# Gated linear attention and a mixture of experts on one core: score steps in four quarters, sums of squares in pieces, and the first expert tile's head inside the last attention slot

## The reference

```python
q = _l2norm((x @ Wq).reshape(Bb, Tt, H, DK))
k = _l2norm((x @ Wk).reshape(Bb, Tt, H, DK))
v = (x @ Wv).reshape(Bb, Tt, H, DV)
alpha = jax.nn.sigmoid(x @ Wg).reshape(Bb, Tt, H, DK)

def step(S, qkva):
    q_t, k_t, v_t, a_t = qkva
    S = a_t[..., None] * S + k_t[..., None] * v_t[:, :, None, :]
    o_t = jnp.einsum('bhkv,bhk->bhv', S, q_t)
    return (S, o_t)
...
x = _layernorm(x + o @ Wo)
x = _layernorm(x + ffn(x))
```

## Time and profile before

| | |
|---|---|
| time, median of 3 runs | 1812.88 us (1812.57 to 1818.45) |
| the profiled execution | 1823.8 us, span 1822.0 us |
| TensorE, matmuls | 1699.3 us busy (93%), 35591 |
| TensorE, weight loads | 1401.9 us busy (77%), 35591 |
| VectorE | 1453.9 us busy (80%), 3326 |
| ScalarE | 1074.1 us busy (59%), 2352 |
| GpSimd | 610.8 us busy (34%), 470 |
| instruction queue | 283 packets, 4.64 MB |

### The profile page before, as it was taken

The page is one execution under the profiler, slowest core; times in us unless marked ns, Lnnn a source line. Parts: engine busy times, 40 slices in busy tenths (PEclk is TensorE's granted clock), DMA queues, the critical chain, the costliest instruction groups (busy, mean ns, idle before and its releaser), DMA issues.

```text
span 1822.0 us, 81575 instructions
## 1 busy us (share of the span) xinstructions
PE 1699.3 (93%) x35591; PEld 1401.9 (77%) x35591; DVE 1453.9 (80%) x3326; ACT 1074.1 (59%) x2352; POOL 610.8 (34%) x470
## 2 busy tenths in 40 slices
PE   6999999999999999999999999999978999999996
PEld 5888878878888788887887888878857777777775
DVE  4888788787878888787877887877857888888886
ACT  5666555655665556655665565655536666666663
POOL 3322232232322232232323222222204554555544
PEclk9999999999999999999999999999989999999998
DMA  7000000000000000000000000000002322223311
GB/s 215 4 9 10 3 10 3 10 4 10 4 9 10 3 9 4 9 4 9 3 10 9 4 9 4 9 4 9 4 14 98 116 82 94 105 71 117 103 67 64
DMA packets 38129, 60.80 MB, mean 33 GB/s; under 512 B 3080, under 2 KB 24848, under 8 KB 37776
## 3 DMA queue, kind: packets, MB, share of 16 engines
q1 hardware_dynamic: 37776, 55.59, 9.1%
HBM read 46.93 MB, written 4.46 MB: 28 GB/s over the span
## 4 chain that ended last, share of the span: by engine, by line
PE 68%; DVE 14%; issue 8%; ACT 5%; DMA 3%; DVEq 0%; POOL 0%; SPq 0%; ACTq 0%; POOLq 0%
PE bank L539 8%; PE bank L672 8%; PE bank L627 7%; PE bank L541 7%; PE bank L540 7%; PE bank L682 5%; PE bank L658 5%; PE bank L630 5%; PE bank L579 5%; PE bank L589 4%; PE bank L646 3%; DVE kt_sb L1510 3%; PE bank L615 3%; DVE v_sb L1517 3%; DMA ew_raw<-cw_dram 2%
## 5 line engine op out<-in xcount | busy, mean ns | idle before, releaser
L471 POOL TENSOR_TENSOR rn_sb<-ss_sb,expo 128x8 f32<-128x8 f32 x128 | 213.5, 1668 | 785.1 <-DVE ss_sb L1272 785.1
L1227 DVE TENSOR_TENSOR qq_sb<-qq_sb,tot_sb 128x512 f32<-128x512 f32 (+1 forms) x384 | 264.5, 689 | 188.1 <-PE bank L627 149.5
L1227 DVE TENSOR_TENSOR k_sb<-k_sb,tot_sb 128x512 f32<-128x512 f32 (+1 forms) x384 | 321.9, 838 | 5.3 <-PE bank L630 5.1
L997 ACT ACTIVATE at_sb<-diag_sb 32x256 f32<-32x256 f32 x256 | 106.0, 414 | 170.6 <-DVE diag_sb L1239 165.9
L972 ACT ACTIVATE v_sb<-bank,rn_sb 128x128 f32<-128x128 f32 x512 | 139.7, 384 | 83.0 <-PE bank L541 80.1
L627 PEld LDWEIGHTS bank<-qq_sb,k_sb 128*32 128x32 f32 x12288 | 128.7, 110 | 58.4 <-issue 43.6
L627 PE MATMUL bank<-qq_sb,k_sb 128*32 128x16 f32 x12288 | 149.8, 185 | 22.3 <-issue 20.5
L961 ACT ACTIVATE a_sb<-bank 128x512 f32<-128x512 f32 x128 | 76.5, 598 | 154.2 <-PE bank L541 145.6
L672 PE MATMUL bank<-v_sb,at_sb 128*128 128x128 f32 x1024 | 151.5, 291 | 5.0 <-issue 2.5
L539 PE MATMUL bank<-wg_hi,ew_hi 128*128 128x512 f32 x320 | 135.2, 423 | 20.1 <-DVE v_sb L1517 20.1
L507 POOL TENSOR_TENSOR wq_lo<-v_sb,wq_hi 128x512 fp32r<-128x512 f32 x80 | 111.9, 1403 | 114.4 <-ACT wq_hi L1120 114.4
(11 more groups left out here) (191 smaller groups left out, 4291.0 us busy)
## 6 DMA issues: line engine op xcount, KB each, us to landing
ew_raw<-cw_dram SPq DMA_DIRECT2D x32, 768.0 KB, 6.4
x_nat<-in_L_attn_x_dram SPq DMA_DIRECT2D x16, 256.0 KB, 3.1
x_nat<-x_all SPq DMA_DIRECT2D x16, 256.0 KB, 2.5
ew_raw<-cw_dram SPq DMA_DIRECT2D x16, 256.0 KB, 3.7
e_sb<-cw_dram SPq DMA_DIRECT2D x16, 256.0 KB, 7.1
out_dram<-k_sb SPq DMA_DIRECT2D x16, 256.0 KB, 2.3
ew_raw<-in_L_ffn_exp_w_dram SPq DMA_DIRECT2D x3, 512.0 KB, 5.1
qq_sb<-in_L_attn_Wq_dram SPq DMA_DIRECT2D x1, 512.0 KB, 3.7
```

What stands on the lines that cost most here:

```text
L471: nc.gpsimd.tensor_tensor(rn_sb[par][:, i, :, :].rearrange("p h c -> p (h c)"), ss_sb[:, i * G:(i + 1) * G], expo[:, 0:G], ALU.pow).then_i ...
L1227: return nc.vector.tensor_tensor(view, view, by, ALU.mult)
```

## The change

Step 6 keeps its matmul count but puts its outputs into all four quarters (even and odd blocks apart), step 7 is cut in two matmuls of 32 columns per block and likewise spread. Step 7 gets bank 7 (`su_ps`) for itself, and the other steps alternate between the banks 2 and 3 in a fixed way, so that their waits change: step 1 waits for the copies of the step 6 before, no longer of step 7; step 7 waits for the clamped sums of the next pair, and state update 0 for the copies of step 7. ScalarE copies step 6 in four instructions and step 7 in two. `sums_of_squares` is called per head: queries behind projection 2 and behind state update 1, keys before and behind `spread_norms`. In the last slot (`end`) TensorE, ScalarE and VectorE run tile 0's `head_x`, `head_z`, `head_gate`, and the first expert's first product; behind it the rest of the first two experts, and the choice of experts; the last sequence's layer norm is applied after the tenth expert of tile 0, and the head of tile 1 is shifted by one to two experts. The banks of tile 0's head are 0, 1 and 5, and its activations lie in `q_sb`.

```diff
-        WIDTH = {0: HB, 1: SB, 3: HB, 4: HB, 5: HB, 6: SB, 7: 2 * SB}
+        WIDTH = {0: HB, 1: SB, 3: HB, 4: HB, 5: HB, 6: SB // 2, 7: SB}
...
-            return sc[(par * STEPS + ORDER.index(j) + 1) % 2][:, 0:G * WIDTH[j]]
+            bank = su_ps if j == 7 else sc[(ORDER.index(j) + 1) % 2]
+            return bank[:, 0:G * WIDTH[j]]
...
-                    await_count(pe, sc_act, P * 3)
+                    await_count(pe, sc_act, P * ACTS - 2)
...
-                pe.wait_ge(sc_evac, P * EVACS + {3: 1, 4: 3, 5: 4, 6: 5, 7: 6}[j])
+                if j < 7:
+                    pe.wait_ge(sc_evac, P * EVACS + {3: 1, 4: 3, 5: 4, 6: 5}[j])
+                elif has_next:
+                    pe.wait_ge(ss_evac, 2 * (P + 2))
+                else:
+                    pe.wait_ge(s_done, P * HP * (NC - 1))
...
-                    for n in range(NB if j < 6 else C // (2 * m)):
+                    for n in range(NB if j < 6 else 2):
...
-                            mm = nc.tensor.matmul(out[2 * m * n:2 * m * n + m, g * m:(g + 1) * m],
-                                                  k_sb[par][:, left:left + m], qd_sb[par][:, left + m:left + 2 * m],
-                                                  start=True, stop=True)
+                            row = ((g % 2 + 2 * n) if j == 6 else (2 * (g % 2) + n)) * SB
+                            keys = g * C + (2 * m * n if j == 6 else SB * n)
+                            queries = g * C + (2 * m * n if j == 6 else 0) + m
+                            mm = nc.tensor.matmul(out[row:row + SB, g // 2 * m:(g // 2 + 1) * m], k_sb[par][:, keys:keys + SB],
+                                                  qd_sb[par][:, queries:queries + m], start=True, stop=True)
...
+                    pe.wait_ge(sc_act, (P + 1) * ACTS)
...
                     if has_next:
                         project(next_p, P + 1, wk, 2)
+                        sums_of_squares(P + 1, 0, 0, n_x)
                     if has_prev:
                         state_updates(1 - par, P - 1, 0)
                     scores(par, P, 3)
                     if has_prev:
                         state_updates(1 - par, P - 1, 1)
                     if has_next:
+                        sums_of_squares(P + 1, 0, 1, n_x)
                         project(next_p, P + 1, wk, 3)
-                        sums_of_squares(P + 1, 0, n_x)
                     scores(par, P, 4)
+                    if end:
+                        head_z(0)
...
                     if has_next:
-                        sums_of_squares(P + 1, 1, n_x)
+                        sums_of_squares(P + 1, 1, 0, n_x)
                         spread_norms(1 - par, P + 1)
+                        sums_of_squares(P + 1, 1, 1, n_x)
                     scores(par, P, 6)
...
-            for h in range(HP):
-                transposes_of_k(P % 2, P, h, last=True)
+            transposes_of_k(P % 2, P, 0, last=True)
+            up_gate(0, 0, 1)
+            transposes_of_k(P % 2, P, 1, last=True)
             for h in range(HP):
                 state_updates(P % 2, P, h)
+                up_linear(0, 0, h)
+            weights_t(0)
...
             for h in range(HP):
                 take_kT(B * NP - 1, h)
+            silu_expert(0, 0)
             first_states(B * NP - 1)
...
+            silu_expert(0, 1)
+            take_weights_t(0)
...
+            rank_experts(0)
+            finish_ranks(0)
+            choose(0)
             states(P % 2, P)
+            for e in range(2):
+                gate_expert(0, 0, e)
             dve.wait_ge(av_done, B * NP * HP)
             ln_halves(B - 1, y3, x_rows(B - 1))
             ln_variance(B - 1)
-            ln1_apply(B - 1)
```

More of the change, by code:

```diff
@@ new lines, in head_gate, with weights_t @@
+            def head_gate(n, par):
+                pe.wait_ge(v_xt32, n + 1)
+                await_count(pe, a_ct, n)
+                for c in range(NC):
+                    mm = nc.tensor.matmul(head_banks(n)[2][:, c * C:(c + 1) * C], xt32_of(n)[:, c * C:(c + 1) * C], gate_t[:, :],
+                                          start=True, stop=True)
+                mm.then_inc(f_gate, 1)
+            def weights_t(n):
+                pe.wait_ge(v_comb, n + 1)
+                for c in range(NC):
+                    mm = nc.tensor.transpose(head_banks(n)[2][0:E, c * C:(c + 1) * C], comb[:, c, :], ident[:, :])
+                mm.then_inc(f_ct, 1)
@@ L715, in _ @@
             mm.then_inc(fold_pe, 1)
-            sums_of_squares(0, 0, 1)
+            for h in range(HP):
+                sums_of_squares(0, 0, h, 1)
             pe.wait_ge(fold_sb, 4)
@@ L732, in _ @@
             pe.wait_ge(fold_bias, 1)
-            sums_of_squares(0, 1, 1)
+            for h in range(HP):
+                sums_of_squares(0, 1, h, 1)
             spread_norms(0, 0)
@@ L748, in body @@
                     scores(par, P, 1)
+                    end = last and p == NP - 1
                     if has_prev:
                         transposes_of_k(1 - par, P - 1, 0)
+                    if end:
+                        head_x(0)
                     if has_next:
```

474 lines of the change are left out of this document (247 added, 227 removed).

## The result

The changed kernel takes 1804.62 us against 1818.41 us for the kernel before on the same chip: 13.8 us less, a ratio of 0.9926 [0.9908, 0.9944]. The forecast was 1765 us, 48 less, and its rivals A and D carried the range up to 1795. The profiled execution has a span of 1800.8 us, against 1822.0.

| piece of the span | before | after | forecast |
|---|---|---|---|
| first to last step 0 (63 slots) | 1292.7 | 1280.3 (−12.4) | −38 |
| last step 0 to the third expert's first matmul | 39.95 | 26.2 (−13.8) | −15 |
| from there to the end | 461.2 | 466.7 (+5.5) | 0 |

A forecast was written before the change was run, and what follows sets the result against it. Attention was taken as bound by TensorE's order of work, VectorE next. Attention's 38 us and the transition's 15 made 53; 48 off the 1812.88 us median gave 1765 us, own range 1750 to 1780, up to 1795 with rivals A and D.

The forecast's parts named there:

- A: Rival for the attention stage: spreading the sums wins nothing, the breaks just move; 1785 us, chance 0.15.
- D: Rival for steps 6 and 7: the quarters don't overlap as said; 1775 to 1790 us, chance 0.09.
- TensorE's prices: TensorE's work per attention slot: step 6 saves 0.26 us, step 7 0.54, spread sums cost 0.58; together -0.22 us.
- The layer-norm slot: One attention slot in four, where VectorE has almost no waits: it gains only 0.3 us.
- The breaks: Gaps inside TensorE's attention blocks, read as late instructions: spreading the sums saves 0.5 us a slot, bounds 0 and 0.8.
- The other three of four: Attention slots without the layer norm: VectorE keeps slack there, so each gains 0.72 us; mean over all slots 0.61.
- C: Slower rival: sums pieces ahead of step 3 put VectorE's chain on the path in every slot; 1835 us, chance 0.04.
- The bank of its own: Attention: step 1 no longer waits for ScalarE's copy of step 7; gain 0, at most 19.1 us.
- ScalarE's three more copies: Steps 6 and 7 in attention: about 0.5 us a slot more on ScalarE, covered by its waits, so cost 0.
- The transition: From attention to experts: the third expert can start right behind attention; 15 us saved, bounds 8 and 19.
- the shift of tile 1's head: Expert stage: costs nothing while VectorE has room in the earlier steps.
- Time against trace: Whole run: 48 us instead of 53 taken off the median, since part of the profiled execution's breaks may be the profiler's.

## Why the prediction was wrong, step by step

- **TensorE's prices were right.** Step 6 takes 0.39 us to the next block (forecast 0.37); step 7 0.57 in the median, 0.47 at the least (0.54); a detached query piece 0.36; a state update behind one 0.87 (0.86). The layer-norm slot gained least, as forecast: its two stretches sum to 20.55 us before and after; the others got 0.14 to 0.25 us shorter.
- **The breaks nearly halved**, from 52.9 to 30.3 us, 0.36 us a slot where 0.5 was taken. That the breaks are late instructions, which the prediction only inferred, the traces bear out (see the last section). But TensorE's idle time in the first stretch fell only from 0.45 to 0.32 us; the rest of what was saved lies in the second, where it counts no longer. The rule that a block's boundary is "mostly hidden" (the Trainium skill, Runtime: NRT & Kernel Launch, Instruction fetch mechanics) is not borne out in full: 30 us of breaks stay even so. It does hold for most packets: some 260 landed in this stretch of either trace, and there were 67 breaks over 0.25 us before and 49 after.
- **The step that failed:** "The other three of four keep slack on VectorE, which waits for steps 3 to 5 ... over 2 us a slot; they gain 0.22 + 0.5 = 0.72". The waits were there, and still are. They lie in the stretch before step 5, and what VectorE must do behind step 5 can't start earlier because of them. In the stretch behind it VectorE had only some 0.6 us to give in three slots of four (9.24 to 8.63) and 0.12 in the layer-norm slot (9.48 to 9.36). A wait was read as slack of the whole slot. What VectorE could give was the 0.50 us between its last product and step 1, and the first stretch took 0.35 of it back, in which the queries' pieces alone cost 0.42 by their distances: 0.13 us a slot were left where 0.61 were forecast. Of 38 us the attention edits together gave 3 us (0.9926 against 0.9944, intervals that overlap) and 0.7 us of trace.
- **The rival that was nearest is C**, in its mechanism: VectorE's chain is on the path in 98% of the slots, with the pieces ahead of step 3 in the other stretch. Its price was wrong: I charged the pieces (0.65 us) and credited none of the quarters and breaks; they pay for the pieces and a little more.
- **VectorE's wait for the queries' sums** fell from 31.1 to 5.0 us, which the sum did not have. It won nothing: the wait lies in the first stretch, and VectorE's idle time there stayed at 3.5 us a slot.
- **The bank of its own** gave nothing in time that can be told from zero: the kernel with both attention edits undone is 0.56% faster than before, 10 us, and its transition and expert stage are worth 11.5 us by its trace (14.3 less 2.8). In the same trace its attention is 11.7 us shorter than before's; some 5 us of it can be before's high profiled execution, and whether the rest is the bank no run tells. ScalarE's three more copies stayed hidden.
- **The transition** was right in its gain, 13.8 us for 15: table loads and silu as expected, and the third expert 0.6 us behind attention's last block instead of 2 to 4. Its cover failed: "the shift of tile 1's head costs nothing while VectorE has the earlier steps' room". It cost 5.5 us in this trace, and the run with the choice one expert earlier gave 6.0 back; other kernels with the same late choice lost between nothing and 5.0 us against before's 461.2.
- **Time against trace:** I took 5 us off because the profiled execution of before stood above the median; it stands 5.4 us above the new one.

Summed: 12.4 + 13.8 − 5.5 + 0.6 = 21.2 us of trace (rounded), and 13.8 of median. What stays open: how much of attention's 12.4 us is the bank of its own and how much the high profiled execution of before, and what besides the late choice lengthened the expert stage.

## What to carry over

Cut the loop at the places where the engines hand the path to each other, and sum each engine's work per stretch: a saving counts only in a stretch that its engine sets, and a wait in another stretch is no slack for it. Before a block is moved past a wait, follow what hangs on its result through every engine: a clamp that came 2.3 us later, with the clock that fell behind its wait, made the kernel 6% slower. One cheap probe, a dummy operation on the engine in doubt, tells whether it is the bound.

## What the runs showed of the hardware

**GpSimd stretches VectorE's operations.** VectorE's growth of k takes 0.69 us alone and 1.53 in the slot above, where it starts at 714.34. GpSimd's timeline there:

```profile
713.87 1.46 POOL L323 TENSOR_TENSOR tot_sb<-a_sb 128x512 f32<-128x512 f32 x1 [2.61 <-DVE s_sb L1321]
...
719.12 0.62 POOL L323 TENSOR_TENSOR tot_sb<-tot_sb 128x256 f32<-128x256 f32 x1
```

GpSimd's product ends at 715.33, and VectorE's operation 0.54 us later, at 715.87, as if it had stood still until about then. The Trainium skill (SBUF — State Buffer, SBUF: two separate sides) says that the two share a port pair that is "an exclusive lock, not a bandwidth split", and that a VectorE operation with two SBUF inputs falls under it. The trace agrees, and the runs with the products on VectorE showed the price: 1.28 us a slot on VectorE (0.84 and 0.44) for products that take 1.1 us there (0.68 and 0.42).

**A late packet of instructions stops TensorE.** The traces record the landing of each 16 KB packet of the instruction queue. Of breaks over 0.25 us inside blocks there are 67 in the stretch of before and 49 in that of after, and every one of them ends 1.19 to 1.59 us behind the landing of a packet; of all matmuls only 14% and 11% start 1.15 to 1.65 us behind one. So matmuls behind such a break started when their instructions had come.

**What a block costs apart and together.** The queries' sums take 0.59 us to the next block in one piece and 0.36 twice in two, and the state updates beside them 0.87 us each instead of 0.76 and 0.69: 0.42 us more apart. The keys' pieces take 0.36 and 0.27 us, as much as the 0.64 of one block, and with their breaks 0.80 us in the mean against 1.00 (before). Which of the two wins depends on whether TensorE sets the stretch.

**Small matmuls over four column quarters**: the rows of one block, two for each float32 matmul, start 0.009 us apart at 16 and at 32 columns and 0.014 at 64 (step 7). Over two quarters it was 0.016 at 32 columns (step 6 before), and in one quarter 0.061 at 64 (step 7 before).

**The granted clock falls with a wait, and the price comes behind it.** The 3.18 us wait for tile 1's choice was followed by 5.4 us at 1.2 GHz, in which a pass takes 0.43 us instead of 0.23 from start to start. Behind the 1.09 us wait of the kernel with the earlier choice the clock stayed at 2.4 GHz.
